# Summing the experts' outputs and forming the second queries inside the second attention, pair by pair

## The reference

```
x = x + attention0(layernorm(x), context, mask)
x = x + experts(layernorm(x))      # top 4 of 32 experts a token, plus a shared one
x = x + attention1(layernorm(x), context)
x = x + binary_ffn(layernorm(x))   # 256 -> 1024 -> 1024 -> 256, weights of +1 and -1
```

## Time and profile before

| | us |
|---|---|
| median of 3 runs (1292.6 to 1301.44) | 1300.81 |
| the profiled execution | 1299.66 |
| its span, first to last instruction | 1297.9 |
| last instructions of the experts to the first fetch of `combine` | 707.4 to 713.1 |
| `combine` | 713.1 to 789.3 |
| second attention | 789.6 to 951.2 |
| last feed-forward layer | 952.5 to the end |

### The profile page before, as it was taken

The page is one execution under the profiler, slowest core; times in us unless marked ns, Lnnn a source line. Parts: engine busy times, 40 slices in busy tenths (PEclk is TensorE's granted clock), DMA queues, the critical chain, the costliest instruction groups (busy, mean ns, idle before and its releaser), DMA issues. The chain is left out here.

```text
span 1297.9 us, 26060 instructions
## 1 busy us (share of the span) xinstructions
PE 1170.6 (90%) x8528; PEld 812.3 (63%) x8528; DVE 743.6 (57%) x1969; ACT 516.6 (40%) x1110; POOL 411.7 (32%) x513
## 2 busy tenths in 40 slices
PE   7799988886998999999996268999989999999998
PEld 4378777664655778777785135888745545554554
DVE  4177877773733566666564784888843343424331
ACT  6555644442211345433442265666532122212221
POOL 5360255554563455555455365100000000000000
PEclk9899998986998999999998598999999999999999
DMA  9199421212297454454451930000000000000000
GB/s 184 12 270 390 150 73 66 73 65 96 81 202 242 155 154 147 148 163 147 126 156 36 389 138 13 2 2 3 2 1 1 17 17 17 9 7 16 17 17 17
DMA packets 100993, 123.93 MB, mean 95 GB/s; under 512 B 34224, under 2 KB 76291, under 8 KB 100871
## 3 DMA queue, kind: packets, MB, share of 16 engines
q1 hardware_dynamic: 87047, 87.98, 23.5%
q0 software_dynamic: 13824, 34.38, 7.6%
HBM read 61.78 MB, written 64.72 MB: 97 GB/s over the span
## 5 line engine op out<-in xcount | busy, mean ns | idle before, releaser
L1981 PE MATMUL psA<-H,B 128*128 128x512 f16 x1024 | 223.5, 379 | 0.0
L1908 DVE SCALAR_TENSOR_TENSOR H<-psA,H 128x512 f16<-128x512 f32 x128 | 88.3, 690 | 209.9 <-ACT H L1949 209.9
L1667 POOL DMA_INDIRECT y_rows<-YB,pair x160 | 155.5, 972 | 148.4 <-DVE YB L1722 82.3
L1949 ACT ACTIVATE H<-psA 128x512 f16<-128x512 f32 x128 | 76.4, 597 | 254.3 <-PE psA L1981 254.3
L1981 PEld LDWEIGHTS psA<-H,B 128*128 128x128 f16 x1024 | 100.3, 98 | 119.2
L1777 PE MATMUL psH<-W,XT 128*128 x640 | 169.5, 388 | 0.8 <-ACT XT L1679 0.8
L944 ACT ACTIVATE PHT<-psT 128x512 f16<-128x512 f32 (+1 forms) x192 | 94.7, 525 | 128.0 <-PE psT L1012 126.3
L866 DVE TENSOR_TENSOR PLT<-psT,PHT 128x512 f16<-128x512 f32 (+1 forms) x192 | 114.1, 597 | 34.2 <-ACT PHT L944 30.6
L208 POOL TENSOR_SCALAR var<-mv 128x4 f32<-128x4 f32 x24 | 11.2, 468 | 372.7 <-DVE mv L202 371.7
L1170 POOL DMA_INDIRECT x_rows<-B,slot_s x96 | 96.3, 1003 | 76.0 <-issue 22.2
L1777 PEld LDWEIGHTS psH<-W,XT 128*128 128x128 f32 x640 | 111.3, 194 | 12.3 <-issue 3.1
(11 more groups left out here) (248 smaller groups left out, 2065.7 us busy)
## 6 DMA issues: line engine op xcount, KB each, us to landing
XG<-x_rows SPq DMA_DIRECT2D x160, 134.0 KB
y_rows<-zero_row SPq DMA_DIRECT2D x4, 4096.0 KB, 27.4
G<-y_rows SPq DMA_DIRECT2D x7, 2048.0 KB, 10.2
x_rows<-zero_row SPq DMA_DIRECT2D x33, 134.0 KB, 8.1
X<-in_x SPq DMA_DIRECT2D x8, 512.0 KB
QT<-in_w SPq DMA_DIRECT2D x16, 256.0 KB
out_x<-OUT SPq DMA_DIRECT2D x8, 512.0 KB
y_rows<-YB,pair POOLq DMA_INDIRECT x160
```

What stands on the lines that cost most here:

```text
L1667: pool.indirect_dma_start(y_rows[:, :], bass.IndirectOffsetOnAxis(ap=pair[u // HALF][:, u % HALF:u % HALF + 1], axis=0), YB[u][:], None, b ...
L1908: dve.scalar_tensor_tensor(out=H[layer][1][:, o], in0=psA[k % 4][:], scalar=0.0, in1=H[layer][0][:, o], op0=ALU.max, op1=ALU.subtract).the ...
L1981: last = pe.matmul(psA[k % 4][:], W[:, c, o * P:(o + 1) * P], src[part][:, c], start=n == 0, stop=n == 2 * n_in - 1)
```

## The change

`combine` is gone. A class `Feed` does its work by pairs of tiles (16 pairs, 1 MB of rows each) inside the second `attend`. The rows of the first three pairs go to parts of `QT` that are free by then, and SyncE issues their fetches at the end of its list in `experts`, ahead of `retire`; the other thirteen go to four buffers `G`. VectorE makes all additions (`by_vector` is always true, so `halve` on GpSimd is never issued) and the statistics: pairs 0 to 2 ahead of the first maxima, pair p from 3 on at the end of body 2p - 6. ScalarE normalises pair p in body 2p - 5, TensorE transposes it in body 2p - 4 and makes the products in body 2p - 3 (pairs 0 and 1 ahead of body 0, pair 2 in bodies 0 and 1), both between the transposed context and the values and in the banks `psT`; ScalarE copies both out at the end of its body. The products have 256 columns instead of 512. GpSimd does its four small steps for a pair and then the bias additions of the pair before. Scores of tile 2p wait for the queries of pair p.

```diff
@@ -58,7 +58,11 @@
 KEYS_AT = 1
 HALF = AHEAD // 2
 LOADS = 8
-GBUFS = 3
+PAIRS = TILES // 2
+PW = 2 * P
+FIRST = 3
+GBUFS = 4
+ADD_AT, APPLY_AT, FEED_TURN_AT, FEED_PRODUCT_AT = -6, -5, -4, -3
...
-    def combine(w):
...
+    def first_rows(p):
+
+        lo = (MT - 1 - p) * 2 * MW
+        return QT[:, :, lo:lo + 2 * MW]
+
+    def outputs_of(p):
+
+        return y_rows[p * PW * TOPK:(p + 1) * PW * TOPK, :].rearrange("(t p k) d -> p t (k d)", p=P, k=TOPK)
+
+    def fetch_first(sp, fetched):
+        for p in range(FIRST):
+            sp.dma_start(first_rows(p), outputs_of(p)).then_inc(fetched[p], 16)
+
+    class Feed:
...
+            self.G = [space(st, "G", [P, 2, TOPK * D]) for _ in range(GBUFS)]
+            self.XN = [space(st, "XN", [P, 2, D]) for _ in range(2)]
+            self.XT = [space(st, "XT", [P, KC, PW]) for _ in range(2)]
...
+        def due(self, t, k, first):
+
+            p, rest = divmod(t - k, 2)
+            return [p] if rest == 0 and first <= p < PAIRS else []
+
+        def rows(self, p):
+            return first_rows(p) if p < FIRST else self.G[(p - FIRST) % GBUFS][:]
...
+        def fetch(self, sp):
+            for p in range(FIRST, PAIRS):
+                if p - GBUFS >= FIRST:
+                    sp.wait_ge(self.summed, p - GBUFS + 1)
+                sp.dma_start(self.rows(p), outputs_of(p)).then_inc(self.fetched[FIRST + (p - FIRST) % GBUFS], 16)
...
+        def add(self, dve, p):
+            x, g = X[:, 2 * p:2 * p + 2, :], self.rows(p)
+            if self.by_vector(p):
+                self.landed(dve, p)
+                for k in range(TOPK - 1):
+                    self.own.done(dve.tensor_tensor(x, x, g[:, :, k * D:(k + 1) * D], ALU.add))
+                last = g[:, :, (TOPK - 1) * D:TOPK * D]
...
+            dve.tensor_tensor(x, x, last, ALU.add).then_inc(self.summed, 1)
+
+        def by_vector(self, p):
+            return True
...
+        def stats(self, dve, p):
+            u = p % 2
+            dve.wait_ge(self.summed, p + 1)
+            if p >= 2:
+                dve.wait_ge(self.shift_ready, p - 1)
+            for i in range(2):
+                last = dve.bn_stats(self.st6[u][:, i, :], X[:, 2 * p + i:2 * p + i + 1, :])
+            last.then_inc(self.stats_out, 1)
+            dve.wait_ge(self.stats_out, p + 1)
+            for i in range(2):
+                last = dve.bn_aggr(self.mv[u][:, i, :], self.st6[u][:, i, :])
+            last.then_inc(self.var_ready, 1)
...
+        def apply(self, act, p):
+            act.wait_ge(self.shift_ready, p + 1)
+            if p >= 2:
+                act.wait_ge(self.turned, p - 1)
+            for i in range(2):
+                last = act.activation(self.XN[p % 2][:, i:i + 1, :], X[:, 2 * p + i:2 * p + i + 1, :], ACT.Identity,
+                                      bias=self.shift[p % 2][:, i:i + 1], scale=self.rstd[p % 2][:, i:i + 1])
+            last.then_inc(self.xn_ready, 1)
...
+        def turned_out(self, act, p, src):
+            act.wait_ge(self.turned, p + 1)
+            if p >= 2:
+                act.wait_ge(self.q_done, p - 1)
+            act.activation(self.XT[p % 2][:], src, ACT.Copy).then_inc(self.x_out, 1)
...
+        def out(self, act, p, src):
...
+            act.wait_ge(self.q_done, p + 1)
+            for o in range(KC):
+                act.activation(QT[:, o, p * PW:(p + 1) * PW], src[:, o], ACT.Identity,
...
+        def turn(self, pe, p, dst):
+            pe.wait_ge(self.xn_ready, p + 1)
+            for c in range(KC):
+                for i in range(2):
+                    last = pe.transpose(dst[:, c, i * P:(i + 1) * P], self.XN[p % 2][:, i, c * P:(c + 1) * P], ident[:])
+            last.then_inc(self.turned, 1)
+
+        def products(self, pe, p, dst):
+            if p == 0:
+                pe.wait_ge(self.wq_ready, KC)
+            pe.wait_ge(self.x_out, p + 1)
+            for o in range(KC):
+                for c in range(KC):
+                    last = pe.matmul(dst[:, o], self.WQ[:, c, o * P:(o + 1) * P], self.XT[p % 2][:, c],
+                                     start=c == 0, stop=c == KC - 1)
+            last.then_inc(self.q_done, 1)
...
-    def attend(w, masked, clear_outputs, load_ahead, tail=None, gate=None):
-        st = ExitStack()
+        feed = Feed(st, w, fetched) if fetched else None
...
-        TURNS = []
+        TURNS = [(feed, p, k) for p in range(FIRST - 1) for k in ("turn", "product")] if feed else []
         for t in range(TILES + 3):
             TURNS += [(t, g) for g in range(NG) if t < TILES]
+            if feed:
+                TURNS += [(feed, p, "turn") for p in feed.due(t, FEED_TURN_AT, FIRST - 1)]
+                TURNS += [(feed, p, "product") for p in feed.due(t, FEED_PRODUCT_AT, FIRST - 1)]
...
-                if earlier[2:] == ("logits",):
+                if earlier[2:] == ("turn",):
+                    pe.wait_ge(feed.x_out, earlier[1] + 1)
+                elif earlier[2:] == ("product",):
+                    pe.wait_ge(feed.q_out, KC * (earlier[1] + 1))
...
+                if feed:
+                    feed.load(sp)
                 sp.dma_start(wo[:], w["wo"].rearrange("(c p) n -> p c n", p=P)).then_inc(loaded, 16)
                 sp.dma_start(bo[:], w["bo"].rearrange("(o n) -> o n", o=1).to_broadcast([P, D])).then_inc(loaded, 16)
+                if feed:
+                    feed.fetch(sp)
...
+                if feed:
+                    for p in range(PAIRS + 1):
+                        if p < PAIRS:
+                            feed.power(pool, p)
+                        if p == 1:
+                            pool.wait_ge(loaded, 32)
+                        if p:
+                            pool.wait_ge(feed.xn_ready, p)
+                            for t in (2 * p - 2, 2 * p - 1):
+                                add_bias(t)
...
+                    if feed:
+                        for p in feed.due(t, ADD_AT, FIRST):
+                            feed.add(dve, p)
+                            feed.stats(dve, p)
+                if feed:
+                    feed.begin(dve)
+                    for p in range(FIRST):
+                        feed.add(dve, p)
+                        feed.stats(dve, p)
                 for h in range(2):
                     maximum(0, 0, h)
...
+                    if feed:
+                        for p in feed.due(t, FEED_TURN_AT, FIRST - 1):
+                            feed.turned_out(act, p, feed_piece(p, "turn"))
+                        for p in feed.due(t, FEED_PRODUCT_AT, FIRST - 1):
+                            feed.out(act, p, feed_piece(p, "product"))
+                        for p in feed.due(t, APPLY_AT, FIRST):
+                            feed.apply(act, p)
+                if feed:
+                    feed.weights(act)
+                    feed.apply(act, 0)
+                    feed.turned_out(act, 0, feed_piece(0, "turn"))
+                    feed.out(act, 0, feed_piece(0, "product"))
+                    feed.apply(act, 1)
+                    feed.turned_out(act, 1, feed_piece(1, "turn"))
                 act.wait_ge(padded, 2)
                 for h in range(2):
                     exps(0, 0, h)
+                if feed:
+                    feed.out(act, 1, feed_piece(1, "product"))
+                    feed.apply(act, 2)
                 steady(body, lambda t: tail and tail.scalar(act, t - TILES))
...
                 def scores(t, u):
                     b = t // BT
+                    if feed and t % 2 == 0:
+                        pe.wait_ge(feed.q_out, KC * (t // 2 + 1))
...
+                    if feed:
+                        for p in feed.due(t, FEED_TURN_AT, FIRST - 1):
+                            feed_turn(p)
+                        for p in feed.due(t, FEED_PRODUCT_AT, FIRST - 1):
+                            feed_products(p)
                     if ok(t - 1):
                         values(t - 1, 1 - u)
...
+                def feed_turn(p):
+                    bank_free(pe, (feed, p, "turn"))
+                    feed.turn(pe, p, feed_piece(p, "turn"))
+
+                def feed_products(p):
+                    bank_free(pe, (feed, p, "product"))
+                    feed.products(pe, p, feed_piece(p, "product"))
+                if feed:
+                    feed_turn(0)
+                    feed_products(0)
                 scores(0, 0)
+                if feed:
+                    feed_turn(1)
                 for h in range(2):
                     shift(0, 0, h)
+                if feed:
+                    feed_products(1)
                 for t in range(TILES + 3):
                     body(t, t % 2)
         st.close()
@@ -1611,7 +1777,7 @@
...
+    def experts(W13, W2, w_loaded, plan_all, own_f, binary, gate, fetched):
...
                 for u in range(AHEAD):
                     sp.wait_ge(stored[u], 16 * ETILES // AHEAD)
+                fetch_first(sp, fetched)
...
```

(34 more changed lines are left out.)

51 lines of the change are left out of this document (added).

## The result

| | us |
|---|---|
| kernel after, median of 4 runs (1326.13 to 1337.95) | 1331.51 |
| kernel before, median of 4 runs (1292.6 to 1301.44) | 1300.43 |
| ratio after / before, with its 95% interval | 1.0258 [1.0197, 1.0318] |
| span of the profiled execution, after | 1336.2 |

A forecast was written before the change was run, and what follows sets the result against it. TensorE was taken as full in the second attention, VectorE as nearly so. Opening -56.2, even tiles +52.0, odd +26.0, last two +2.6 sum to +24.4 us: 1299.66 becomes 1324, own range 1311 to 1340, 8 in 10 1296 to 1343.

The forecast's parts named there:

- Even tiles: Second attention, tiles 0 to 24: a pair's sum on VectorE makes 8.6 us instead of 4.61; 13 times 4.0, 52.0 us more.
- Odd tiles at full clock: Second attention, tiles 1 to 25: a pair's products on TensorE delay values and scores; 6.6 us, 13 times 2.0, 26.0 more.
- the wait before the reciprocal: Sign in odd tiles: VectorE idles some 2.5 us there, for the values; its absence would refute the forecast.
- T: The moment at which VectorE has made a tile's maxima and turns to the low parts.
- long VectorE tiles and long TensorE tiles add and don't average: Second attention: they stand one behind the other, so a pair of tiles takes 15.2 us where it took 9.2.
- the 1.18 us wait of the first attention: Sign from before: eight transposes inserted at this spot on TensorE made VectorE wait 1.18 us for the values.
- rival C: TensorE's clock falls after 2.5 us waits per pair, doubling some 4 us in odd tiles: 52 more, 1376 us; chance 0.08.
- the forecast's 80.6: Loss forecast over the second attention's tiles: 52.0 us in even ones, 26.0 in odd ones, 2.6 in tiles 26 and 27.
- Tiles 26 and 27: End of the feeding: transposes alone in tile 26, 0.6 us, products alone in tile 27, 2.0; together 2.6 more.
- The opening: From the experts' end to the second attention's first tiles: early fetches and only the first pairs' work ahead, 56.2 us gained.
- the reset, taken as 1.3 us: Reset between experts and attention: the first fetches, issued before it, start about 1.3 us earlier, at 711.8.
- What was costed at nothing: Second attention: thirteen further fetches, ScalarE's 2.6 us more per pair of tiles, GpSimd's small steps and bias additions; no cost.

## Why the prediction was right, and where it wasn't

**Even tiles: right.** 8.6 us predicted, 8.51 measured, with the cause named: all of VectorE's sum stands in the period. Leaving out two additions took exactly their time (1.45 us) off it.

**Odd tiles at full clock: right.** 6.6 predicted, 6.62 measured; the wait before the reciprocal 2.5 predicted, 2.34 measured. Its inner times came true as well: products at T + 1.65 and scores at T + 4.35 predicted, 1.67 and 4.36 measured (T is 829.54, 1.41 us after the maxima at 828.13). That it is the products' place in TensorE's order is shown from two sides: behind the scores, 4.53; behind the values, 6.34. The step that long VectorE tiles and long TensorE tiles add and don't average, carried the forecast's sign, and the 1.18 us wait of the first attention was a fair sign of it.

**The clock: wrong.** The step that failed is the dismissal of rival C: "in the summing stage TensorE waited 2.44 us in each group, and ... the clock was 1.00", hence 1.00 in the middle. It fell in ten of thirteen pairs, after one wait of 3.05 us and nine of eleven waits of 2.21; it stayed up after the other two and after the one of 1.95. The price given with C failed too: not 4 us of TensorE work at half speed but part of it, 1.5 us a tile. In the tile shown the shift at 812.18 still runs at full speed (0.53 us for two, as at 828.98), and only the products and the values behind them are slow. Ten tiles make 14.9 us. The loop took 12.7 more than the forecast's 80.6: those 14.9, less 2.9 because the even tiles came out shorter (tiles 0 and 2 took 7.4 and 7.9), and 0.7 spread over the rest. (Tiles 26 and 27 took 2.7 more, 2.6 predicted.) Filling the idle time, shortening it by less VectorE work, or using it for early products each brought 1.00 back from tile 3 on. The Trainium skill, "TensorE: Matmul & The Clock Gate", section "🎯 Why this matters for your kernels", warns of idle gaps between bursts of matmuls; it was on C's side, and the runs agree with it in ten of the thirteen pairs, not in the other three. Why a wait of 2.21 us leaves the clock up in two pairs, one of 2.44 did so in the summing stage, while one of 1.69 brought it down in tile 1 with two additions left out, stays open: no run set the length of the wait by itself.

**The opening: mis-sized, on the safe side.** 56.2 predicted, 61.3 measured. The term that was wrong is the reset, taken as 1.3 us from the one behind the attention: here fetching ahead of it saves 4.5 us. The price of the one place was taken for the other. The table of before bounded it from above, 5.7 us from the experts' last instructions to the first fetch (707.4 to 713.1), of which 1.2 are the wait for the stores that stays (712.46 to 713.68 in after), and it wasn't used. Why the two resets differ no run shows. The forecast also let the three issues delay the reset's end by 1.35 us; they delay it by nothing. What follows the first addition was well sized: 15.8 us to the first maxima predicted, 15.96 measured (718.82 to 734.78). Pair 1's products, costed at 1.5 us behind the first scores, cost nothing: 4.96 us from the first to the second maxima, 5.54 before. The 5.1 us are 3.2 from the reset and 2.1 from pair 1, less 0.2.

**What was costed at nothing** was nothing: no fetch is late in the attention (5.1 us each), and no engine waits for GpSimd's steps in the tiles. VectorE waits for ScalarE about once a pair, 0.70 us before the even tile's last low part, where it waited 0.54 before.

Two errors of opposite sign, 5.1 us too little gained and 12.7 too little lost, leave 7.6 of the 32.0 unforecast. The mechanism of the two kinds of tile was right; that the total came as close as 7.6 us is in part luck, because the two errors partly cancel.

## What to carry to other kernels

In this pipeline work that left its own stage cost its full time wherever no other engine's piece ran over it; before placing such work, ask which instruction stands behind it on that engine and who waits for that. Here eight matmuls, moved by a few places in one list with their copies in another, were worth 3.8% of the whole time. Where a change makes TensorE wait, price its clock too, on the work that comes shortly after the wait, and test it by filling the wait with matmuls whose result is overwritten.

## What the runs showed of the hardware

- TensorE's granted clock fell to 0.50 after idle times of 2.21 us, a little after work had begun again: shift at full speed, products 3.58 us instead of 1.99. Within one kernel, two of eleven such idle times left it at 1.00, and so did one of 1.95 us; in another run one of 1.69 us brought it down.
- 32 matmuls of 128 columns on bf16 that nobody reads, in 13 tiles, made the kernel 1.4% faster.
- The same reset has no one price. Behind the experts GpSimd stands 5.73 us from its last scatter to its next instruction, and a fetch issued inside that time comes 4.5 us earlier; behind the attention TensorE starts 1.3 us after the last addition has ended. Three issues on SyncE (1.41 us) inside the reset don't lengthen it.
- GpSimd's addition of two float32 operands of 128x512 took 1.27 us, VectorE's 0.69. The Trainium skill, "GPSIMD Engine Reference", section "4.1 Engine selection", has it about twice as slow; the trace agrees (1.84).
